# Weight chunks and K/V reloads issued from ScalarE's queue in a fused gated cross-attention block, with the lines of all engines reordered

## What is computed

```python
n = layernorm(x)
q = rope(n @ Wq); k = rope(ctx @ Wk); v = ctx @ Wv      # 32 heads of q, 8 of k and v, D = 128
s = where(mask == 0, -1e9, q @ k.T / sqrt(128))
a = softmax(s) @ v
x = x + tanh(g_xattn) * (a @ Wo)
x1, x2 = split(layernorm(x) @ w12.T + b12)
x = x + tanh(g_ffn) * ((silu(x1) * x2) @ w3.T + b3)
```

## Time and profile before

| what | value |
|---|---|
| median of 3 runs | 637.25 us (635.72 to 639.18) |
| the profiled execution | 636.77 us, of which the trace spans 634.9 us |
| TensorE (PE) | busy 623.6 us, 98% of the span |
| VectorE (DVE), GpSimd (POOL), ScalarE (ACT) | 482.8, 450.3 and 319.2 us |
| DMA queues | 57.7% of 16 engines' span on SP's queue (q1) |
| exchanges p | 51 stores and 51 loads of 256 KB, median 2.1 and 3.4 us to landing |
| exchanges s | 48 stores and 48 loads of 256 KB, median 2.2 and 3.4 us |

### The profile page before, as it was taken

One profiled execution on the slowest core, in us unless ns is written; L12 is line 12 of the kernel. 1 busy time (PEld: TensorE's weight loads), 2 busy tenths in 40 slices (PEclk: granted clock), 3 DMA queues, 4 the chain that ended last, 5 costly groups with the idle time before them and its releaser, 6 DMA issues.

```text
span 634.9 us, 10094 instructions
## 1 busy us (share of the span) xinstructions
PE 623.6 (98%) x2865; PEld 511.7 (81%) x2865; DVE 482.8 (76%) x1235; ACT 319.2 (50%) x893; POOL 450.3 (71%) x374
## 2 busy tenths in 40 slices
PE   8999999998999999999999999999999999999997
PEld 7888888876888877787888788888778788888886
DVE  3987675797878878788878788878885998976342
ACT  5435622554764646455455555554634657545310
POOL 6456866898889898888898898988886677601100
PEclk9999999999999999999999999999999999999999
DMA  9997995156587686776677676876645413000002
GB/s 300 324 324 227 295 321 166 70 188 211 178 266 230 201 249 207 240 244 213 196 244 241 211 245 221 261 234 213 216 139 176 131 50 90 0 2 1 0 34 99
DMA packets 133990, 118.38 MB, mean 186 GB/s; under 512 B 9776, under 2 KB 104496, under 8 KB 133936
## 3 DMA queue, kind: packets, MB, share of 16 engines
q1 hardware_dynamic: 132512, 116.69, 57.7%
q0 software_dynamic: 384, 1.05, 0.5%
q10 hardware_dynamic: 1040, 0.00, 0.1%
HBM read 72.89 MB, written 44.83 MB: 185 GB/s over the span
## 4 chain that ended last, share of the span: by engine, by line
PE 69%; DVE 9%; POOL 8%; DMA 7%; issue 4%; ACT 3%; DVEq 0%; POOLq 0%; ACTq 0%; SPq 0%
PE f_bank L889 9%; PE f_bank L891 9%; PE f_bank L890 9%; PE o_bank L889 7%; PE o_bank L891 7%; PE o_bank L890 7%; DMA p<-p_scratch 3%; DVE t_sin L2417 3%; PE pv_bank L889 3%; PE pv_bank L891 3%; PE pv_bank L890 3%; PE s_banks L889 2%; PE s_banks L891 2%; PE s_banks L890 2%; ACT prob L1492 2%
## 5 line engine op out<-in xcount | busy, mean ns | idle before, releaser
L1492 ACT ACTIVATE prob<-prob,small 128x128 f32<-128x128 f32 x256 | 99.6, 391 | 42.0 <-DVE small L2516 27.9
L889 PE MATMUL f_bank<-xT_hi,wq_hi 128*128 128x512 f32 x256 | 100.4, 392 | 0.7 <-DVE t_sin L2417 0.6
L891 PE MATMUL f_bank<-xT_hi,wq_lo 128*128 128x512 f32 x256 | 99.8, 390 | 0.0
L890 PE MATMUL f_bank<-xT_lo,wq_hi 128*128 128x512 f32 x256 | 99.8, 390 | 0.0
L889 PE MATMUL o_bank<-wo_hi,o_hi 128*128 128x512 f32 x248 | 97.9, 395 | 0.5 <-issue 0.4
L891 PE MATMUL o_bank<-wo_hi,o_lo 128*128 128x512 f32 x248 | 97.0, 391 | 0.0
L890 PE MATMUL o_bank<-wo_lo,o_hi 128*128 128x512 f32 x248 | 96.7, 390 | 0.0
L2004 POOL TENSOR_TENSOR q<-t_cos,t_sin 128x512 f32<-128x512 f32 x64 | 83.2, 1304 | 14.1 <-DVE t_sin L2417 13.7
L2417 DVE TENSOR_TENSOR t_sin<-f_bank,rope 64x512 f32<-64x512 f32 x128 | 88.1, 688 | 2.3
L1964 POOL TENSOR_TENSOR q_lo<-q,q_hi 128x512 fp32r<-128x512 f32 x64 | 82.9, 1297 | 9.5 <-ACT q_hi L1422 9.3
L2019 POOL TENSOR_TENSOR pT_lo<-p,pT_hi 128x512 fp32r<-128x512 f32 x51 | 66.2, 1297 | 22.3 <-ACT pT_hi L1422 22.3
(11 more groups left out here) (185 smaller groups left out, 1439.4 us busy)
## 6 DMA issues: line engine op xcount, KB each, us to landing
p_scratch<-p_blk SPq DMA_DIRECT2D x51, 256.0 KB, 2.1
p<-p_scratch SPq DMA_DIRECT2D x51, 256.0 KB, 3.4
s_scratch<-s_blk SPq DMA_DIRECT2D x48, 256.0 KB, 2.2
s<-s_scratch SPq DMA_DIRECT2D x48, 256.0 KB, 3.4
k_scratch<-ks_parts SPq DMA_DIRECT2D x16, 512.0 KB, 3.1
raw<-in_L_xattn_Wq_dram SPq DMA_DIRECT2D x32, 256.0 KB, 3.9
raw<-in_L_xattn_Wo_dram SPq DMA_DIRECT2D x32, 256.0 KB, 3.5
k_parts<-k_scratch SPq DMA_DIRECT2D x16, 512.0 KB, 4.6
```

What stands on the lines that cost most here:

```text
L889: nc.tensor.matmul(dst, st[0], mv_[0], start=start, stop=False)
L890: nc.tensor.matmul(dst, st[0], mv_[1], start=False, stop=False)
L891: return nc.tensor.matmul(dst, st[1], mv_[0], start=False, stop=stop)
L1492: e = nc.scalar.activation(prob[:, k, h, :], prob[:, k, h, :], ACT.Exp, bias=nmin[k][:, h:h + 1], scale=-1.0, accum_out=psum_row[k][:, h:h ...
```

## The change

`load_k`, `load_v`, `load_chunk`, `next_k`, `next_v` and `load_next_chunk` of the attention are written for ScalarE (`act`) in place of SP, and all their calls stand in ScalarE's list: 47 chunk loads, 14 reloads of K and 14 of V (two DMAs each), 89 DMAs. One chunk load (`load_chunk(0, 2)`) and all those before the attention stay on SP. `next_k` and `next_v` also wait for the stores of K and V of the first stage, which SP had waited for. In SP's list the exchanges, `ffn_load`, the biases and the output stay. The lists of all engines are reordered; no computation is added or taken away.

```diff
@@ block.sync
-            load_next_chunk(0)
             load_chunk(0, 2)
-            next_k(0, 1)
-            load_next_chunk(1)
             store_p(*u(2))
             store_s(4)
-            load_next_chunk(2)
             load_p(*u(2))
             load_s(4)
+            store_s(5)
             store_p(*u(3))
-            store_s(5)
             load_s(5)
-            load_next_chunk(3)
-            load_next_chunk(4)
             load_p(*u(3))
...
             store_p(*u(49))
             store_s(51)
+            load_p(*u(49))
             load_s(51)
-            load_p(*u(49))
             ffn_load(0)
@@ block.tensor
             scores(0, 0, 1)
             prob_transpose(0, 0, 0)
             q_block(0, 6)
+            scores(0, 1, 0)
             pv(0, 0, 0)
-            scores(0, 1, 0)
             q_block(0, 7)
             prob_transpose(0, 0, 1)
+            scores(0, 1, 1)
             q_block(0, 8)
-            scores(0, 1, 1)
             q_block(0, 9)
...
             q_block(0, 11)
+            scores(*u(6))
             pv(*u(2))
-            scores(*u(6))
             out_proj(*u(1))
+            out_proj(*u(2))
             scores(*u(7))
-            out_proj(*u(2))
             pv(*u(3))
...
             q_block(0, 47)
+            scores(*u(43))
             out_proj(*u(38))
             pv(*u(39))
-            scores(*u(43))
             q_block(0, 48)
@@ block.scalar
+            def load_chunk(o, G):
+
+                act.wait_ge(pool_wlo, pool_split(16 + 8 * (G - 1) + o))
+                dst = raw[:, o, :]
+                if o < 4:
+                    dst = dst.rearrange("p (t c) -> p t c", t=KT)
+                act.dma_start(dst, wq_src(G, o) if o < 4 else wo_src(G, o - 4)).then_inc(raw_loaded[o], 16)
+
+            def next_k(half, G):
+                act.wait_ge(pe_score, 8 * (G - 1) + 4 * half + 4)
+                act.wait_ge(k_stored[half], 8 * KBLOCKS)
+                load_k(half, G)
+
+            def next_v(half, G):
+                act.wait_ge(pe_pv, 8 * (G - 1) + 4 * half + 4)
+                for slot in range(4):
+                    act.wait_ge(v_stored[slot], v_stores(slot, 16))
+                load_v(half, G)
...
             exps(*u(41))
-            pT_hi_copy(*u(40))
+            load_next_chunk(39)
+            next_v(1, 5)
             q_hi_copy(*u(44))
             o_hi_copy(*u(39))
```

More of the change, by code:

```diff
@@ L1155, in _ @@
             scores(*u(9))
+            out_proj(*u(4))
             q_block(0, 14)
-            out_proj(*u(4))
+            pv(*u(6))
             scores(*u(10))
+            q_block(0, 15)
             out_proj(*u(5))
-            pv(*u(6))
-            q_block(0, 15)
             pv(*u(7))
+            scores(*u(11))
             out_proj(*u(6))
-            scores(*u(11))
             q_block(0, 16)
+            out_proj(*u(7))
             scores(*u(12))
-            out_proj(*u(7))
             pv(*u(8))
@@ L1181, in _ @@
             q_block(0, 20)
-            out_proj(*u(11))
             pv(*u(12))
             scores(*u(16))
+            out_proj(*u(11))
             q_block(0, 21)
+            pv(*u(13))
             out_proj(*u(12))
-            pv(*u(13))
             scores(*u(17))
             q_block(0, 22)
+            q_block(0, 23)
             pv(*u(14))
+            scores(*u(18))
             out_proj(*u(13))
-            scores(*u(18))
-            q_block(0, 23)
             pv(*u(15))
@@ L1230, in _ @@
             out_proj(*u(23))
+            scores(*u(28))
             pv(*u(24))
-            scores(*u(28))
             q_block(0, 33)
-            out_proj(*u(24))
-            pv(*u(25))
             scores(*u(29))
             q_block(0, 34)
+            pv(*u(25))
+            out_proj(*u(24))
+            scores(*u(30))
             out_proj(*u(25))
-            scores(*u(30))
             pv(*u(26))
@@ L1330, in _ @@
             pv(*u(49))
+            q_block(0, 58)
             out_proj(*u(48))
@@ L1336, in _ @@
             pv(3, 1, 0)
-            q_block(0, 58)
+            scores(3, 2, 1)
             q_block(0, 59)
             pv(3, 1, 1)
-            scores(3, 2, 1)
             out_proj(3, 1, 0)
             out_proj(3, 1, 1)
+            scores(3, 3, 0)
             pv(3, 2, 0)
-            scores(3, 3, 0)
             q_block(0, 60)
@@ L1565, in mask_columns, with load_k, load_v, load_next_chunk @@
                    mfill[:, HB * half:HB * half + HB, :].rearrange("p b (a j) -> p b j a", j=4), act_mask2)
+            def load_k(half, group):
+                act.dma_start(f32(k_parts[:, half].rearrange("p b k -> p (b k)")),
+                             k_dram[bass.ds(group * 256 + half * 128, 128), :]).then_inc(k_loaded[half], 16)
+            def load_v(half, group):
+                for t, part in enumerate((v_hi, v_lo)):
+                    act.dma_start(f32(part[:, half].rearrange("p b d -> p (b d)")),
+                                 v_dram[bass.ds(group * 256 + (2 * half * KVH + t) * 128, 128), :]).then_inc(v_loaded[half], 16)
+            def load_chunk(o, G):
[13 more added lines that the diff above has]
+                load_v(half, G)
+            def load_next_chunk(n):
+                G, r, k = n // 8, n // 2 % 4, n % 2
+                if k == 0 and G + 2 < KVH:
+                    load_chunk(2 * r + 1, G + 2)
+                elif k == 1 and r < 3 and G + 2 < KVH:
+                    load_chunk(2 * r + 2, G + 2)
+                elif k == 1 and r == 3 and G + 3 < KVH:
+                    load_chunk(0, G + 3)
             def h_norm(b):
@@ L1681, in _ @@
             split_chunk(*pair_chunks(*u(18)[:2])[0])
+            next_v(1, 2)
             o_hi_copy(*u(15))
@@ L1764, in _ @@
             o_hi_copy(*u(31))
+            next_v(1, 4)
             exps(*u(34))
@@ L1822, in _ @@
+            o_hi_copy(*u(43))
             q_hi_copy(*u(48))
-            o_hi_copy(*u(43))
+            q_hi_copy(*u(49))
+            load_next_chunk(44)
+            pT_hi_copy(*u(44))
             exps(*u(46))
-            pT_hi_copy(*u(44))
+            split_chunk(*pair_chunks(*u(47)[:2])[1])
+            next_v(0, 6)
+            q_hi_copy(*u(50))
             o_hi_copy(*u(44))
-            q_hi_copy(*u(49))
+            load_next_chunk(45)
             pT_hi_copy(*u(45))
+            split_chunk(*pair_chunks(*u(48)[:2])[0])
@@ L2690, in _ @@
             sin_q(15)
+            o_lo_split(*u(7))
             p_blocks(*u(9))
```

894 lines of the change are left out of this document (436 added, 458 removed).

## The result

The change makes the kernel slower: 650.92 us median of 4 runs (648.19 to 653.29) against 638.0 us of the kernel before in the same comparison, a ratio of 1.0211 (95% interval 1.0183 to 1.0240), clear of no change. The forecast was 634.0 us, with a range from 628.5 to 640.0.

What follows compares the result with a forecast made beforehand. TensorE, busy 623.6 of 634.9 us, was taken as the bound, with 6.3 us of idle time in the attention to gain. −2.9 − 0.4 + 0.5 = −2.8 us against 636.8 us gave 634.0 us, range 628.5 to 640.0.

Steps and rivals of the forecast that it cites:

- The start, −2.9 us: Attention from 114 to 160 us: the new order fills four TensorE waits, −2.9 us (bounds −3.9 and 0).
- The gaps before the pv of unit 2 and the scores of unit 7: Start of the attention: waits of 0.92 and 0.97 us, to be filled or covered by other matmuls.
- the wait for t_sin: Start of the attention: 0.6 us before a q_block, which would now have the scores of unit 3 ahead.
- The end, −0.4 us: 460 to 545 us: the p load of unit 49 goes about 0.5 us sooner, −0.4 us (bounds 0 and −0.6).
- The middle ... cost the reorder there at nothing. The cover is that operands are ready ahead of TensorE: 160 to 460 us: reorder costed at nothing, as TensorE idles for only 1.8 of 260 us from 200 to 460.
- not for an exchange: 160 to 460 us: longest waits, 1.0 us in two, read as pv waiting for the previous unit's o_lo.
- Transfers ... I take 0, since the bytes are the same: Landing of the p loads: no change in time taken, 0 us in the sum.
- The bound of 0.7 us for each load: p loads: each could land 0.7 us sooner, median to the least, or later by as much.
- ScalarE's 89 issues at nothing: ScalarE in the attention: 89 issues at 0.48 us, 43 us, busy from 55% to 66%, mean costed at nothing.
- The rival on them: ScalarE's issues delay o_hi and TensorE by 0.48 us at up to 20 units: 643.6 us (+1.0%); chance 0.12.
- `next_v(1, 5)`, +0.5 us: ScalarE waits for unit 39's pv, delaying o_hi 1.1 us ahead of its out_proj: +0.5 us (bounds 0 and +1.3).
- where I expected nothing: Behind 545 us, after the attention: no DMA changes its queue, so no change in time expected.

Runs made afterwards that it cites:

- lists_from_sp: Kernel after with its reordered lists, but the 89 DMAs issued from SyncE at the moments ScalarE had issued them; 644.53 us, ratio 1.0148 to the kernel before.
- old_act_small: Kernel before with its old lists, the 89 DMAs issued from ScalarE and the bytes of chunk, K and V loads cut; 633.49 us, ratio 0.9944.
- old_small_all: Kernel before, DMAs still on SyncE, with the bytes of chunk, K and V loads cut; 632.51 us, ratio 0.9941.
- old_with_new_start_long: Kernel before with the new order on all engines up to about unit 10 to 12, DMAs on SyncE; 635.08 us, ratio 0.9979.

## Why the prediction was wrong

- **The start, −2.9 us: right in the main.** 2.1 us of idle time were gained. The gaps before the pv of unit 2 and the scores of unit 7 are gone, and the p load of unit 3 is issued 2.0 us behind its store, as forecast; the wait for t_sin stayed (0.5 us), and 0.3 us before some scores. It was the order that did it, not the queue: lists_from_sp, with the chunk loads on SP, issues that load as early and idles for 0.96 us there as well.
- **The end, −0.4 us: not borne out.** Idle time from 460 to 545 us fell from 1.4 to 0.3 us, but the kernel after is some 14 us late by then, so the stretch holds other work. The p load of unit 49 did go sooner behind its store (2.1 in place of 3.3 us); the gap before its pv went from 0.37 to 0.26 us only.
- **"The middle ... cost the reorder there at nothing. The cover is that operands are ready ahead of TensorE": this step failed.** The cost was 11.6 us more idle time from 200 to 460 us and, over the span, 4.5 us more busy time, which goes with the restarts behind gaps and the lower clock. The text named the cover and did not check it, and it misread a row. It took the waits for o_lo for waits "not for an exchange". The longest of them in the kernel before, followed back past VectorE to ScalarE, is one: o_hi stood behind the pT_hi that waited for a p load (ScalarE, VectorE, TensorE):

```profile
291.49 0.63 ACT L1422 ACTIVATE pT_hi<-p 128x512 fp32r<-128x512 f32 x1 [3.96 <-DMA p<-p_scratch]
...
293.07 0.58 ACT L1422 ACTIVATE o_hi<-pv_bank 128x512 fp32r<-128x512 f32 x1
...
293.68 0.69 DVE L2370 TENSOR_TENSOR o_lo<-pv_bank,o_hi 128x512 fp32r<-128x512 f32 x1 [0.46 <-ACT o_hi L1422]
...
294.52 0.47 PE L889 MATMUL pv_bank<-pT_hi,v_hi 128*128 128x512 f32 x1 [0.73 <-DVE o_lo L2370]
```

TensorE was full there, but some of its operands came just in time, by way of an exchange.
- **"Transfers ... I take 0, since the bytes are the same": the term that was mis-sized.** The bytes are the same, but the place of each against the exchanges is not. The bound of 0.7 us for each load was about right for the mean of a load with transfers ahead and behind it (3.71 to 4.51 us); but the prediction never asked how many loads it could hit, took the p loads alone where more of the loss came through the s loads, and carried none of it into the sum or a rival.
- **ScalarE's 89 issues at nothing: right as far as is shown.** An issue took 0.39 us on average and not 0.48. old_act_small has them all and runs at 633.5 us; with full transfers no run separates them. The rival on them had the sign and, by chance, near half of the size, but not the mechanism.
- **`next_v(1, 5)`, +0.5 us: near in size, but by luck.** The gap is there, 0.81 us before the out_proj of unit 39. But its o_hi waited for something else: the q_hi of unit 44 ahead of it stood until 424.19 for GpSimd's q, when the two DMAs had been issued by 423.46. lists_from_sp, with these DMAs on SP, has the same gap, 0.80 us. It is the new order of ScalarE that makes it.

```profile
423.00 0.46 ACTq L1474 DMA_DIRECT2D v_lo<-v_scratch  x1
424.19 0.63 ACT L1323 ACTIVATE q_hi<-q 128x512 fp32r<-128x512 f32 x1 [4.92 <-POOL q L2021]
...
424.73 0.58 ACT L1323 ACTIVATE o_hi<-pv_bank 128x512 fp32r<-128x512 f32 x1
...
426.13 0.47 PE L790 MATMUL o_bank<-wo_hi,o_hi 128*128 128x512 f32 x1 [0.81 <-ACT o_hi L1323]
```

- **The queue.** The Trainium skill, *DMA: Bandwidth & Descriptors*, section "Issuing engines are not separate DMA queues", says that transfers of all issuers interleave on the same engines. The trace agrees: the p load of unit 26 and the chunk load that ScalarE issued 0.23 us behind it took 5.95 and 5.92 us and landed 0.2 us apart. I had drawn from it only that nothing is to be gained. What can be lost by it I had not asked: the spacing among the exchanges that the transfers had in SP's queue, where they stood behind its waits. That this is what ScalarE's queue costs fits the runs with moved places, but is argued.
- **Not foreseen:** 2.4 us of idle time behind 545 us, where I expected nothing since no DMA changes its queue there. It was the order of the lists that changed.

What stays open: how the loss of the kernel after divides between the queue, the places and the new lists. At the same lists, moving the DMAs from ScalarE to SyncE at the same moments gained about 4.5 us (+12.9 against +8.4 us), but a moment is the same only to within an instruction, and one place on one queue is worth more than that. Nor is it shown why the new lists lose 8 to 9 us on SyncE's queue, or which of the moved transfers does the damage.

## What to carry to other kernels

A full engine says nothing about the slack of what feeds it. Take even its short waits and follow each back from engine to engine, past what stands ahead in each engine's list, to see whether it ends at a DMA. How often a reader stands at a DMA does not tell it: ScalarE waits for p loads 34 times in the kernel before, 31 times in the kernel after and 30 times in old_small_all, the fastest of all. Where exchanges that others wait for share DMA engines with bulk loads (here 72% busy), the order in an in-order queue is a schedule, and moving bulk loads by one place can cost more than the change was to bring. Two controls tell quickly: the same kernel with the bulk transfers cut to a fraction, and the old kernel with them moved by one place. The first shows that bytes matter, not which order can bear them.

## What the runs showed that had not been expected

- **A DMA issue of ScalarE ran beside its ACTIVATE.** The issue at 310.34 (0.39 us) lies within the copy of 310.32 to 310.95, and the next copy starts at 310.86, 0.54 us behind the first, as copies do with no issue between (0.53 us from 318.01 to 318.54).
- **The clock fell after a wait.** Behind the wait of 2.39 us matmuls started 0.43 us apart, in place of 0.23, for some 3 us. Busy time by stretch of the kernel after:

```profile
320.00:326.00 6.00, 5.41 (x17) 4.33 (x18) 5.44 (x17) 1.55 (x8) 6.00 (x6) 0.72 0.74 243
```

A granted clock of 0.72 over 6 us is the lower of its two levels (1.2 and 2.4 GHz) for a bit over half of them. It fell again behind a wait of 1.9 us at 351.6 (0.66 from 351 to 356), but not behind that of 2.19 us in old_with_new_start_long (1.00 there), so the length of one wait does not decide it alone. A gap can thus cost more than itself.
